# Layer-norm rows of a routing stage split over three engines, and its expert choice batch by batch

## What is computed

```python
h = _layernorm(x, axis=-1) * (1 + cb) + sb
gate_logits = xf @ Wr                      # xf: h as 4096 rows of 256, Wr: 256 x 8
w, idx = jax.lax.top_k(gate_logits, 2)
w = jax.nn.softmax(w, axis=-1)
```

## Time and profile before

| | |
|---|---|
| median of 3 runs | 2876.08 us (2870.78 to 2876.3) |
| profiled execution: time, span | 2874.07 us, 2872.4 us |
| mean granted clock of TensorE | 0.935 |
| TensorE busy | 2483.7 us (86%) |
| VectorE busy | 2102.1 us (73%) |
| ScalarE busy | 1296.7 us (45%) |
| GpSimd busy | 1238.7 us (43%) |
| route of layer 0 | about 970 to 1057 us of the span |

### The profile page before, as it was taken

One profiled execution on the slowest core, in us unless ns is written; L12 is line 12 of the kernel. 1 busy time (PEld: TensorE's weight loads), 2 busy tenths in 40 slices (PEclk: granted clock), 3 DMA queues, 4 the chain that ended last, 5 costly groups with the idle time before them and its releaser, 6 DMA issues.

```text
span 2872.4 us, 38064 instructions
## 1 busy us (share of the span) xinstructions
PE 2483.7 (86%) x12341; PEld 1788.6 (62%) x12342; DVE 2102.1 (73%) x4278; ACT 1296.7 (45%) x2564; POOL 1238.7 (43%) x532
## 2 busy tenths in 40 slices
PE   6677868768776759999699999999999999959998
PEld 4455545545555549999366666666666666747776
DVE  4999999999999756666666667766776667655554
ACT  4677677677675335554233324332433243311111
POOL 2799999999999226666100000020002000233344
PEclk8889989889987879999899999999999999969999
DMA  4645555555557254444400010001001000125554
GB/s 149 195 155 189 169 178 190 167 182 189 163 179 219 75 163 91 63 63 60 125 1 1 1 48 1 1 31 33 1 1 34 15 1 1 67 84 125 128 132 75
DMA packets 151375, 268.84 MB, mean 94 GB/s; under 512 B 18348, under 2 KB 107612, under 8 KB 150844
## 3 DMA queue, kind: packets, MB, share of 16 engines
q1 hardware_dynamic: 122460, 227.12, 25.1%
q0 software_dynamic: 28224, 37.78, 8.1%
q10 hardware_dynamic: 544, 2.10, 0.2%
HBM read 209.52 MB, written 57.43 MB: 93 GB/s over the span
## 4 chain that ended last, share of the span: by engine, by line
PE 45%; DVE 3%; issue 2%; ACT 1%; DMA 1%; POOL 0%; another core or an unknown queue 0%; SPq 0%; DVEq 0%; POOLq 0%
PE at_o_ps L2007 8%; PE at_s_ps L1983 8%; PE at_qk_ps L1965 6%; PE e_h_ps L1584 5%; PE e_y_ps L1595 5%; PE at_s_ps L2015 4%; PE at_pt_ps L1994 4%; PE at_qk_ps L1970 3%; PE at_s_ps L1965 1%; DVE at_small L2384 1%; PE e_x_ps L1573 1%; PE at_s_ps L1970 0%; ACT at_pt L2144 0%; PE at_qk_ps L1903 0%; ACT at_probs L2133 0%
## 5 line engine op out<-in xcount | busy, mean ns | idle before, releaser
L793 POOL TENSOR_TENSOR dbx<-u,b_all 128x2048 f32<-128x2048 f32 x128 | 578.8, 4536 | 71.3 <-DVE u L872 31.6
L1847 POOL DMA_INDIRECT slots<-at_r_rows,slot_of x64 | 64.5, 1008 | 1101.7 <-DVE slot_of L2300 1021.9
L676 ACT ACTIVATE da_ps<-delta,a_neg 128x512 f32<-128x512 f32 x512 | 347.9, 689 | 132.6 <-DVE hc L945 124.3
L2144 ACT COPY at_pt<-at_pt_ps 128x512 f32<-128x512 f32 (+3 forms) x384 | 171.6, 483 | 515.0 <-PE at_pt_ps L1994 508.8
L469 PE MATMUL y_ps<-ident,hc 128*128 128x128 f32 x1536 | 246.8, 306 | 81.9 <-DVE hc L945 81.3
L1983 PE MATMUL at_s_ps<-at_qk 128*128 128x512 f32 (+3 forms) x768 | 290.8, 488 | 0.0
L2007 PE MATMUL at_o_ps<-at_pt,at_v 128*128 128x512 f32 (+3 forms) x768 | 288.4, 487 | 0.0
L469 PEld LDWEIGHTS y_ps<-ident,hc 128*128 128x128 f32 x1536 | 201.6, 158 | 137.0 <-DVE hc L945 108.5
L2133 ACT ACTIVATE at_probs<-at_s_ps,at_small 128x128 f32<-128x128 f32 (+7 forms) x256 | 192.1, 751 | 169.8 <-DVE at_small L2386 166.6
L945 DVE TENSOR_TENSOR hc<-da_ps,c_all 128x512 f32<-128x512 f32 x384 | 256.9, 671 | 0.0
L935 DVE TENSOR_TENSOR_SCAN da_ps<-da_ps,state,dbx 128x512 f32<-128x512 f32 x192 | 242.9, 1274 | 4.5 <-ACT da_ps L676 3.6
(11 more groups left out here) (409 smaller groups left out, 5011.5 us busy)
## 6 DMA issues: line engine op xcount, KB each, us to landing
b_all<-bc_rows SPq DMA_DIRECT2D x128, 512.0 KB, 4.6
c_all<-bc_rows SPq DMA_DIRECT2D x128, 512.0 KB, 5.0
w_qkv<-L_ffn_w SPq DMA_DIRECT2D x32, 512.0 KB
slots<-zeros SPq DMA_DIRECT2D x40, 260.0 KB, 6.5
e_xs<-slots SPq DMA_DIRECT2D x16, 650.0 KB, 7.1
w<-L_ffn_W SPq DMA_DIRECT2D x24, 384.0 KB, 8.8
more<-zeros SPq DMA_DIRECT2D x16, 256.0 KB, 5.1
sums<-x SPq DMA_DIRECT2D x8, 512.0 KB, 7.0
```

What stands on the lines that cost most here:

```text
L676: nc.scalar.activation(da_ps[s % RING_DA][:], delta[:, c % 2, m, :], ACT.Exp, scale=sh.a_neg[:, m, n:n + 1]).then_inc(S["da_ready"], 1)
L793: nc.gpsimd.tensor_tensor(dbx[:, at % RING_DBX], pair, rows, ALU.mult).then_inc(S["dbx_ready"], 1)
```

## The change

A row is made in three steps by three engines. *Normalise*: (x - mean) * rstd, for even tiles on VectorE with one TENSOR_SCALAR, for odd tiles on ScalarE with one ACTIVATE (scale rstd, bias -mean * rstd, which VectorE computes once into `dif`). *Scale*: times (1 + cb), in place, a TENSOR_TENSOR on VectorE. *Add*: plus sb, a TENSOR_TENSOR on GpSimd, into `row8`. The rings and their waits are the same, the waits for a free place in `row8` are now GpSimd's. ScalarE makes tiles 1 and 3 first, and the odd tiles of group g+1 behind the copies of tiles 1 and 3 of group g. VectorE's loop is written out.

The choice of experts is made a batch at a time with 128 x 64 instructions: after the rows of batch b, that of batch b-1; the last one at the end. `score_ready` goes. TensorE's instructions are the same.

```diff
--- before.py
+++ after.py
...
@@ -1094,6 +1094,15 @@
                 nc.gpsimd.iota(dst[:], pattern=pattern, base=base, channel_multiplier=step,
                                allow_small_or_imprecise_dtypes=True).then_inc(consts_ready, 1)
 
+            pool.wait_ge(sh.route_mods_in, 16)
+            for t in range(TILES):
+                b, j = t // TPB, t % TPB
+                pool.wait_ge(half_ready, t + 1)
+                pool.wait_ge(row_turned, t + 1)
+                if j % CT == 0:
+                    pool.wait_ge(rows_copied[j // CT], b * 16 + 1)
+                nc.gpsimd.tensor_tensor(row8[:, j, :], half[:, t % 4, :], sh.mods[:, 0, b, :], ALU.add).then_inc(row_ready, 1)
+
             of_token = lambda b: token[:, b * TPB:(b + 1) * TPB].rearrange("p (t o) -> p t o", o=1).broadcast_to([P, TPB, TILES0])
             for b in range(B):
                 pool.wait_ge(block_hot, b + 1)
@@ -1103,6 +1112,15 @@
         def _(act):
             act.wait_ge(var_ready, 1)
             nc.scalar.activation(sh.var[:], sh.var[:], ACT.Sqrt).then_inc(std_ready, 1)
+            def normalise(t):
+                act.wait_ge(row_ready, t + 1)
+                nc.scalar.activation(half[:, t % 4, :], sh.x[:, t, :], ACT.Identity, bias=sh.dif[:, t:t + 1],
+                                     scale=sh.rstd[:, t:t + 1]).then_inc(odd_ready, 1)
+
+            act.wait_ge(norm_ready, 1)
+            for t in (1, 3):
+                normalise(t)
+
             def copy_turned(t):
                 g = t // GT
                 act.wait_ge(row_turned, t + 1 + TPB)
@@ -1124,12 +1142,12 @@
                 for i in range(GT):
                     if g < GROUPS:
                         copy_turned(g * GT + i)
+                        if i % 2 and g < GROUPS - 1:
+                            normalise((g + 1) * GT + i)
                     if i == 0 and g > CPB and g % CPB == 1:
                         copy_logits(g // CPB - 1)
                     if i == 1 and 1 <= g <= GROUPS:
                         copy_tall(g - 1)
-            act.wait_ge(logits_copied, B)
-            act.sem_inc(score_ready, 1)
             act.wait_ge(gap_ready, 1)
             nc.scalar.activation(sh.weight[:, 1], sh.weight[:, 1], ACT.Exp).then_inc(exp_ready, 1)
             act.wait_ge(consts_ready, 8)
@@ -1184,7 +1202,7 @@
                         turn_back(g - 1)
             product(GROUPS - 1)
             turn_back(GROUPS - 1)
-            pe.wait_ge(masks_ready, 1)
+            pe.wait_ge(masks_ready, B)
             pe.wait_ge(consts_ready, 1)
             nc.tensor.matmul(tri_ps, tri[:], both[:], start=True, stop=True).then_inc(ranked, 1)
             nc.tensor.matmul(tot_ps, ones[:], both[:], start=True, stop=True).then_inc(ranked, 1)
@@ -1207,30 +1225,53 @@
             finish_stats(nc, dve, link, sh, var_ready, std_ready)
             dve.wait_ge(sh.route_mods_in, 16)
 
-            def row_free(b, j):
-
-                dve.wait_ge(row_turned, b * TPB + j + 1)
-                if j % CT == 0:
-                    dve.wait_ge(rows_copied[j // CT], b * 16 + 1)
-
-            norm_rows(nc, dve, sh, half, row8, half_ready, row_ready, row_free)
-
-            over = lambda a: a.rearrange("p (t o) -> p t o", o=1).broadcast_to([P, TILES, NE])
-            dve.wait_ge(score_ready, 1)
-            dve.wait_ge(consts_ready, 8)
-            values = logits
-            for k in range(2):
-
-                link(nc.vector.tensor_reduce(top[:, k], values[:], AX_X, ALU.max))
-                link(nc.vector.tensor_tensor(cand[:], values[:], over(top[:, k]), ALU.is_lt))
-                link(nc.vector.scalar_tensor_tensor(out=cand[:], in0=cand[:], scalar=float(NE), in1=iota_e[:], op0=ALU.mult, op1=ALU.add))
-                chosen = meta[:, :, 3] if k == 0 else idx[:]
-                link(nc.vector.tensor_reduce(chosen, cand[:], AX_X, ALU.min))
-                link(nc.vector.tensor_tensor(mask[:, k], iota_e[:], over(chosen), ALU.is_equal))
-                if k == 0:
-                    link(nc.vector.scalar_tensor_tensor(out=scores[:], in0=mask[:, 0], scalar=-3e38, in1=values[:], op0=ALU.mult, op1=ALU.add))
-                    values = scores
-            nc.vector.tensor_tensor(both[:], mask[:, 0], mask[:, 1], ALU.add).then_inc(masks_ready, 1)
+            nc.vector.scalar_tensor_tensor(out=sh.dif[:], in0=sh.mean[:], scalar=-1.0, in1=sh.rstd[:],
+                                           op0=ALU.mult, op1=ALU.mult).then_inc(norm_ready, 1)
+
+            def normalise(t):
+                dve.wait_ge(row_ready, t + 1)
+                nc.vector.tensor_scalar(half[:, t % 4, :], sh.x[:, t, :], sh.mean[:, t:t + 1], sh.rstd[:, t:t + 1],
+                                        ALU.subtract, ALU.mult).then_inc(even_ready, 1)
+
+            def scale(t):
+                dve.wait_ge(odd_ready if t % 2 else even_ready, t // 2 + 1)
+                nc.vector.tensor_tensor(half[:, t % 4, :], half[:, t % 4, :], sh.mods[:, 1, t // TPB, :], ALU.mult).then_inc(half_ready, 1)
+
+            def halves(b):
+                for t in range(b * TPB, (b + 1) * TPB, 2):
+                    normalise(t)
+                    if t:
+                        scale(t - 1)
+                    scale(t)
+                if b == B - 1:
+                    scale(TILES - 1)
+
+            over = lambda a: a.rearrange("p (t o) -> p t o", o=1).broadcast_to([P, TPB, NE])
+
+            def choose(b):
+                at = slice(b * TPB, (b + 1) * TPB)
+                dve.wait_ge(logits_copied, b + 1)
+                values, c = logits[:, at, :], cand[:, at, :]
+                for k in range(2):
+                    link(nc.vector.tensor_reduce(top[:, k, at], values, AX_X, ALU.max))
+                    link(nc.vector.tensor_tensor(c, values, over(top[:, k, at]), ALU.is_lt))
+                    link(nc.vector.scalar_tensor_tensor(out=c, in0=c, scalar=float(NE), in1=iota_e[:, at, :], op0=ALU.mult, op1=ALU.add))
+                    chosen = meta[:, at, 3] if k == 0 else idx[:, at]
+                    link(nc.vector.tensor_reduce(chosen, c, AX_X, ALU.min))
+                    link(nc.vector.tensor_tensor(mask[:, k, at, :], iota_e[:, at, :], over(chosen), ALU.is_equal))
+                    if k == 0:
+                        link(nc.vector.scalar_tensor_tensor(out=scores[:, at, :], in0=mask[:, 0, at, :], scalar=-3e38, in1=values, op0=ALU.mult, op1=ALU.add))
+                        values = scores[:, at, :]
+                nc.vector.tensor_tensor(both[:, at, :], mask[:, 0, at, :], mask[:, 1, at, :], ALU.add).then_inc(masks_ready, 1)
+
+            for b in range(B):
+                halves(b)
+                if b == 0:
+                    dve.wait_ge(consts_ready, 8)
+                else:
+                    choose(b - 1)
+            choose(B - 1)
+            dve.wait_ge(masks_ready, B)
 
             nc.vector.tensor_tensor(sh.weight[:, 1], top[:, 1], top[:, 0], ALU.subtract).then_inc(gap_ready, 1)
             link(nc.vector.tensor_copy(meta[:, :, 0], token[:]))
```

More of the change, by code:

```diff
@@ L1047, in phase_route @@
         (gate_in, var_ready, std_ready, chain, half_ready, row_ready, row_turned, turn_copied, tall_done, tall_copied, logits_done,
-         logits_copied, consts_ready, score_ready, masks_ready, ranked, gap_ready, exp_ready, meta_ready, meta_stored, lane_hot, block_hot, block_set, second_set, map_done, map_copied, held_done,
+         logits_copied, consts_ready, norm_ready, even_ready, odd_ready, masks_ready, ranked, gap_ready, exp_ready, meta_ready, meta_stored, lane_hot, block_hot, block_set, second_set, map_done, map_copied, held_done,
          pool_chain) = (
             sem(n) for n in ("gate_in var_ready std_ready chain half_ready row_ready row_turned turn_copied tall_done tall_copied logits_done "
-                             "logits_copied consts_ready score_ready masks_ready ranked gap_ready exp_ready "
+                             "logits_copied consts_ready norm_ready even_ready odd_ready masks_ready ranked gap_ready exp_ready "
                              "meta_ready meta_stored lane_hot block_hot block_set second_set map_done map_copied held_done pool_chain").split())
```

## The result

| | before | after |
|---|---|---|
| median (15 runs each) | 2873.61 us | 2880.34 us (2877.91 to 2884.33) |
| profiled execution: time, span | 2874.07, 2872.4 us | 2880.34, 2878.3 us |
| granted clock, mean | 0.935 | 0.935 |
| route: stage's first VectorE work to the map's end | 84.86 us | 91.11 us |

The change makes the kernel slower: ratio 1.0022 [1.0016, 1.0029], +6.7 us. The median lies just beyond 0.2%, the interval reaches to both sides of it. The route takes 6.25 us more (from VectorE's first instruction of the stage at 969.96 to its `gather_i` at 1054.82 before, 971.54 to 1062.65 after), which lies within the interval of the increase, 4.6 to 8.3 us. With 15 runs the median of before is 2.5 us under the one of three runs that the prediction started from.

The account below looks back on a forecast made before the run. The prediction took TensorE's loop of turns and products, running through ScalarE at three places, as the bound, not rows. Terms 0.7 + 3.0 + 3.0 - 2.4 = +4.3 us on 2876.08 gave 2880.4, range 2876.0 to 2886.5.

Parts of the forecast that it names:

- The start: First route, before the first product: new rows at 1.08 us each are slower than TensorE's first turns, +0.7 us.
- ScalarE's share: TensorE's loop: an odd half directly ahead of the 8x512 copy lengthens groups 1 to 6 by 0.50 each, +3.0 us.
- The choice at the end: Behind the last row: only batch 3 is left to choose, 3.05 us instead of 5.46, -2.4 us.
- The choice among the rows: Choices for batches 0 and 1 on VectorE make rows late, delaying the product 1.5 us at two places, +3.0 us.
- What costs nothing: Weights' DMAs, some 6 us later, still end before the stage does; GpSimd's rows precede its map work; TensorE's instruction count unchanged.
- Rival A: Port shared by VectorE and GpSimd decides the pace of rows: +6.3 to +14.6, priced +10, 2886 us; chance 0.25.
- Rival B: Rows never late, ScalarE's half hidden, only the choice at the end counts: -2.4 or -3.4, 2873.7 to 2872.7 us; chance 0.13.

Follow-up runs that it names:

- experiment 1: The change with the choice of experts put back as one 128x256 piece behind all rows, rows still on three engines: 2879.51 us, ratio 1.0009 to before.
- experiment 6: The change plus five identity products on TensorE in the wait ahead of the late turns at each of two places: 2878.89 us, ratio 1.001 to before.
- experiments 2 and 3: Kernel before with only the choice made batch by batch: 2 at the change's places, 3 three tiles later; 2872.96 us (0.9989) and 2872.95 us (0.9991).
- experiment 4: The change with ScalarE's odd halves behind its copies of tiles 2 and 3, none ahead of the 8x512 copy: 2882.79 us, ratio 1.0021 to before.
- experiment 5: The change with each batch's last odd row scaled ahead of the choice, a single run: 2884.2 us beside 2876.19 for the kernel before.
- experiment 7: The change with ScalarE's halves behind its copies of tiles 2 and 3 and each choice three tiles later: 2881.69 us, ratio 1.0015 to before.
- experiment 8: The change with GpSimd's add replaced by a memset, rows not computed, a single run: 2882.68 us beside 2876.19 for the kernel before.

## Why the prediction was right in its sign and form, and where it was not

The predicted 2880.4 and the measured 2880.34 agree by luck: the base, 2876.08, was 2.5 above the median of 15 runs, and the increase was 6.7 (route 6.25) where the sum said 4.3, 2.4 too little. The two errors cancel. By its steps:

- *The start*, +0.7: +0.42. The first five turns took 4.51 us for 4.30. Most of this term was the pace of rows, 1.08 forecast; GpSimd's pairs at 996.06 and 998.00 give 1.94 for two, 0.97 a row. VectorE's TENSOR_SCALAR, taken as 0.35 from another form, is 0.41 alone and 0.81 beside the add.
- *ScalarE's share*, +3.0: 5.46 a group for 4.96, in six groups, and experiment 1 shows it alone. Right.
- *The choice at the end*, -2.4: -2.45. Right. The ranking products were assumed at 1.2 GHz; the clock held (0.6 us on the path), and the map took 0.55 back. In six other kernels with the same idle time it did not hold (below).
- *The choice among the rows*, +3.0: **this term was mis-sized**. Measured: 2 x (7.54 - 5.46 + 6.07 - 5.46) = 5.4. How late the rows make the product was as worked out: with the clock held (experiment 6) the interval is 6.91 for a forecast of 6.93, although the first late turn came 1.26 us late (996.96 for 995.70) and not 1.49, and the second made up the rest. The step that failed is the last one: "its turn takes 0.5", and the product behind it at full speed. In the earlier trace rows I had read that a wait lets the clock fall, and applied it to the ranking alone, not to the new wait that I had just put into the loop. At the lower clock the two turns took 2.08 us for 1.16 and the product 2.47 for 1.88.
- *What costs nothing*: the weights' first DMA went from 1004.31 to 1021.09, 16.8 us later and not 6, since they stand behind the stores of the last rows on SP's queue, and rows, which used to be made far ahead of TensorE, are now stored until 1020.9. It is hidden all the same: the last weights are asked for at 1042, the DMA share is 0.01 from 1055, and `gather_i` comes at 1062.65.

With the four terms as measured the sum is 0.42 + 3.0 + 5.4 - 2.45 = 6.4, for the route's 6.25.

*Rival A* (the port decides the rows, +6.3 to +14.6) comes out near in time and wrong in cause: once the start was over TensorE waited for rows only behind the choices, at 0.97 a row, far from the 1.37 from which A decides. The Trainium skill ("SBUF — State Buffer", Who interferes with whom) says that of VectorE and GpSimd whoever issues first has the SBUF ports that they share for the whole instruction, and that the other is fully blocked. The trace agrees as to the blocking (0.81 for 0.41). It does not agree with adding up whole durations, which is what A did: unblocked ones, 0.41 + 2 x 0.42 + 2 x 0.72, one behind the other, would give 1.34 a row, and 0.97 was measured, so they overlap in part. What part of an instruction blocks the other engine, these runs do not show. *Rival B* did not occur; it is nearly what experiments 2 and 3 are, without the three engines. The chances put 0.67 on no change; the measured median, +0.22%, lies just on the other side, by the clock's 2.4 us (with the clock held it is 1.0010), and its interval reaches to both sides.

## What to carry to other kernels

Work moved off an engine that is not the bottleneck gains nothing, and a piece of it that stands directly ahead of a step for which the loop's chain waits costs its full occupancy, here 0.49 us a group; behind that step the same piece cost nothing in the groups before the first choice (experiment 4). A block of 3 us on one producer fits only where more than 3 us of its product are ahead, so count the ring and the latest producer, not the mean pace. And price a new wait of TensorE with what the clock may do in it or behind it: here 1.2 us of waiting cost 1.2 us more in the work behind.

## What was not expected of the hardware

- The granted clock fell from 1.00 to 0.50 inside a loop in which TensorE already had gaps of 0.97 or 0.48 us a group. Those alone left it at 1.00 in the kernel before and in experiments 1 to 3. At the first of the two places it fell within the new wait of 1.18 us in the change, 1.12 in experiment 5 and 1.43 in experiment 7, but behind the waits of 1.69 in experiment 4 and 0.63 in experiment 8, 1.2 and 0.9 us after TensorE had gone back to work. In the change it was low from 996.8 to about 1000.2, and that cost 1.2 us. In experiment 6, where the waits were filled, it stayed at 1.00 through the loop.
- Ahead of the ranking the same idle time of 3.39 or 3.40 us went different ways: products of 0.70 and 0.64 us in the change, 0.85 and 1.06 in experiment 6, and 1.22 and 1.06, the lower clock throughout, in experiments 2, 3, 4, 5, 7 and 8. Experiment 3 shows such a pair:

```profile
1021.46 1.22 PE L1187 MATMUL rt_wide_ps<-rt_both,rt_tri 128*128 128x256 f32 x2 [3.39 <-DVE rt_both L1238]
...
1022.47 1.06 PE L1188 MATMUL rt_wide_ps<-rt_both,rt_ones 128*128 128x256 f32 x2
```

So the prediction's lower clock there is what most of these kernels show, and the length of a wait alone does not tell what it does to the clock; what does, these runs leave open.
- A faster loop lost to it: in experiment 4 the half microsecond to be won in each of the four groups around the choices went, but for 0.13 us in all, into longer waits and slow products such as the one of 3.40 us.
- VectorE's 128x256 TENSOR_SCALAR takes 0.41 us alone and is recorded with 0.81 beside GpSimd's add, while a pair of rows still comes every 1.94 us. So such a record holds time in which the engine stood blocked.
